# Second attention: where ScalarE's copy of the value products and VectorE's low parts and additions stand in a step

## The reference, cut to what matters

```
q = x @ Wq.T;  k = context @ Wk.T;  v = context @ Wv.T        # 16 heads of 16, context of 154 rows
scores = jnp.einsum('bhqd,bhkd->bhqk', q, k) * SCALE
scores = jnp.where(causal[None, None, :, :], scores, -jnp.inf) # causal = tril(1024 x 154)
probs = jax.nn.softmax(scores, axis=-1)
y = jnp.einsum('bhqk,bhkd->bhqd', probs, v)
return y.transpose(0, 2, 1, 3).reshape(b, t, c) @ Wo.T + bo    # then x + tanh(g) * this
```

## Time and profile before

| | us |
|---|---|
| median of 3 runs | 3179.37 (3177.24 to 3179.78) |
| the profiled execution | 3180.92 |
| its span | 3179.1 |
| second attention in it, first to last score | 2616.5 to 2942.2 |
| busy: PE, DVE, ACT, POOL | 3027.3, 2439.1, 1636.8, 718.9 |

### The profile page before, as it was taken

The page is one execution under the profiler, slowest core; times in us unless marked ns, Lnnn a source line. Parts: engine busy times, 40 slices in busy tenths (PEclk is TensorE's granted clock), DMA queues, the critical chain, the costliest instruction groups (busy, mean ns, idle before and its releaser), DMA issues. The chain is left out here.

```text
span 3179.1 us, 64710 instructions
## 1 busy us (share of the span) xinstructions
PE 3027.3 (95%) x21380; PEld 2785.9 (88%) x21380; DVE 2439.1 (77%) x4983; ACT 1636.8 (51%) x3099; POOL 718.9 (23%) x1290
## 2 busy tenths in 40 slices
PE   5999999999999999999989999999999988999688
PEld 5999999999999999999978888999999987777476
DVE  6777777777777777887876687878878768777797
ACT  3655555555555555555643332222222237777687
POOL 3232222322223322222101111111111122222220
PEclk9999999999999999999999999999999999999899
DMA  3000000000000000000020022334343320000001
GB/s 104 11 15 11 13 12 12 15 11 13 13 10 15 13 12 13 11 11 8 1 61 5 19 69 89 115 94 116 96 116 95 96 80 3 1 0 1 1 21 34
DMA packets 117392, 114.10 MB, mean 36 GB/s; under 512 B 39630, under 2 KB 83078, under 8 KB 117126
## 3 DMA queue, kind: packets, MB, share of 16 engines
q1 hardware_dynamic: 117126, 110.75, 12.1%
HBM read 105.46 MB, written 5.24 MB: 35 GB/s over the span
## 5 line engine op out<-in xcount | busy, mean ns | idle before, releaser
L454 ACT ACTIVATE x_pth<-x_ps 128x512 fp32r<-128x512 f32 (+1 forms) x768 | 375.9, 528 | 254.2 <-PE x_ps L751 251.6
L1107 ACT ACTIVATE moe_sil<-moe_ps,all_b 128x512 f32<-128x512 f32 x256 | 176.1, 688 | 543.8 <-PE moe_ps L1291 541.6
L555 DVE TENSOR_TENSOR x_ptl<-x_ps,x_pth 128x512 fp32r<-128x512 f32 (+1 forms) x768 | 402.9, 552 | 30.9 <-ACT x_pth L454 18.8
L474 ACT ACTIVATE all_buf<-all_buf,x_nmx 128x1178 f32<-128x1178 f32 x256 | 327.6, 1280 | 129.1 <-DVE all_buf L590 128.8
L590 DVE TENSOR_SCALAR_CACHE_REDUCE all_buf<-x_ps 128x1182 f32<-128x1182 f32 x256 | 354.5, 1385 | 22.3 <-PE x_ps L762 13.5
L1316 PE MATMUL moe_ps<-moe_w2z,moe_gh 128*128 128x256 f32 (+1 forms) x1280 | 369.4, 289 | 2.1 <-DVE moe_gl L1241 2.0
L751 PE MATMUL x_ps<-ident,all_buf 128*128 128x128 f32 x2560 | 365.3, 274 | 6.0 <-DVE x_ptl L555 5.9
L1316 PE MATMUL moe_ps<-moe_w2z,moe_gl 128*128 128x256 f32 x1280 | 362.8, 283 | 0.0
L1316 PE MATMUL moe_ps<-moe_w2l,moe_gh 128*128 128x256 f32 x1280 | 362.6, 283 | 0.0
L777 PE MATMUL x_ps<-x_pth,x_vh 128*128 128x256 f32 x1152 | 347.0, 301 | 0.0
L777 PE MATMUL x_ps<-x_ptl,x_vh 128*128 128x256 f32 x1152 | 325.9, 283 | 0.0
(11 more groups left out here) (383 smaller groups left out, 7897.9 us busy)
## 6 DMA issues: line engine op xcount, KB each, us to landing
moe_gate<-moe_cw_rows SPq DMA_DIRECT2D x512, 128.0 KB, 2.9
all_buf<-in_L_ffn_w_dram SPq DMA_DIRECT2D x16, 512.0 KB, 5.7
xres<-in_x_dram SPq DMA_DIRECT2D x4, 1024.0 KB, 10.3
x_rawk<-in_L_xattn_Wkv_dram SPq DMA_DIRECT2D x32, 128.0 KB, 2.2
x_rawq<-in_L_xattn_Wq_dram SPq DMA_DIRECT2D x32, 128.0 KB, 2.2
x_rawv<-in_L_xattn_Wkv_dram SPq DMA_DIRECT2D x16, 256.0 KB, 2.9
x_rawo<-in_L_xattn_Wo_dram SPq DMA_DIRECT2D x32, 128.0 KB, 2.0
out_dram<-xres SPq DMA_DIRECT2D x8, 512.0 KB, 2.9
```

The lines of the kernel that those rows point to most:

```text
L454: act.activation(turn_dst(pth, x, lo, hi), turn_src(x, g), ACT.Copy).then_inc(hi_done, 1)
L474: act.activation(p[:, w % 4, DUP:DUP + R_KV], p[:, w % 4, DUP:DUP + R_KV], ACT.Exp, bias=nmx[:, w % 2:w % 2 + 1], scale=-1.0, accum_out=su ...
L555: last = dve.tensor_tensor(turn_dst(ptl, x, lo, mid), turn_src(x, g)[:, 0:mid - lo, :], turn_dst(pth, x, lo, mid).bitcast(F32), ALU.subtract)
L1107: act.activation(dst[:, q % 2, :], ps[:, HID + q % 2, :], ACT.Silu, bias=bias).then_inc(silu_done, 1)
```

## The change

On ScalarE `keep` moves to the head of the step. On VectorE `maximum` 0, `divide`, `maximum` 1 and `kept` 1 move ahead of `x_part`, `q_part`, the addition and `o_part`; `kept` 2 stays behind them. No instruction is added or taken away.

```
 # ScalarE
             def step(b, w, before, after):
+                keep(b, behind(w, 3, 1, before))
                 if w % 4 == 0 and w < STEPS and (after or w + 4 < STEPS):
                     x_part(CPB * b + w // 4 + 1)
                 if w % 4 == 1 and w < STEPS and (after or w + 3 < STEPS):
                     q_part(CPB * b + w // 4 + 1, (w // 4 + 1) % 2)
                 o_part(b, behind(w, TURN_OUT + 1, 4, before))
-                keep(b, behind(w, 3, 1, before))
                 kept(b, behind(w, 1, 1, before), 0)
 # VectorE
             def step(b, w, before, after):
+                if w < STEPS:
+                    maximum(b, w, 0)
+                divide(b, behind(w, 3, 1, before))
+                if w < STEPS:
+                    maximum(b, w, 1)
+                kept(b, behind(w, 1, 1, before), 1)
                 if w % 4 == 0 and w < STEPS and (after or w + 4 < STEPS):
                     x_part(CPB * b + w // 4 + 1)
...
                 o_part(b, behind(w, TURN_OUT + 1, 4, before))
-                if w < STEPS:
-                    maximum(b, w, 0)
-                divide(b, behind(w, 3, 1, before))
-                if w < STEPS:
-                    maximum(b, w, 1)
-                kept(b, behind(w, 1, 1, before), 1)
                 kept(b, behind(w, 1, 1, before), 2)
```

More of the change, by code:

```diff
@@ L1825, in step @@
                 o_part(b, behind(w, TURN_OUT + 1, 4, before))
[L1826 to L1831, removed]
                 kept(b, behind(w, 1, 1, before), 2)
```

## The result

The changed kernel takes 3197.34 us (median of 6 runs, 3195.76 to 3198.23), the kernel before 3178.3 us in the same comparison (6 runs, 3176.28 to 3184.26). The ratio is 1.0054 with a 95% interval of 1.0044 to 1.0063: slower by 17 us, between 14 and 20. The forecast was slower by 9.2 us. The direction and the mechanism came as forecast, the size is nearly twice the forecast. The median lies 0.3 us above the upper end of the range of 3175 to 3197 us; taken by the ratio from the 3179.37 us that the forecast started from it is 3196.5 us, just inside.

The account below looks back on a forecast made before the run. TensorE was taken to set the pace; two waits go but longer new chains come: +11.5 us in the groups, -2.5 in the first ten steps, +0.2 in the last units, so +9.2 us, 3188.6 us, range 3175 to 3197.

Parts of the forecast that it names:

- The waits that go: TensorE's waits at `tokens` (10.5 us in the stage) and `values` (8.1) removed; 2.06 us off a plain group.
- the four new waits: TensorE behind VectorE's moved instructions: `turn_out` about 0.56 us, `x_turn` and `query` 0.50, `project` 1.20; 2.76 us a group.
- The chain: Last `score` 1 matmul, second maximum, copy, moved part, TensorE's start: 2.39 us in A and B, 2.45 D, 3.09 C.
- "3.09 in C": Chain length in step C, 1.70 us plus 1.39 for the query's low part; TensorE then waits 1.20 us.
- "1.74 us longer": A causal group, with four more score matmuls in each step, goes from 21.49 to 23.23 us.
- "SP and POOL see nothing": No transfer is issued by what moves, so SP and POOL (GpSimd) are unaffected.
- The 48 steps in sum: Eight plain groups 5.6 us, three causal 5.2, one D and A 0.9, one B and C -0.2: +11.5 us.
- The first ten steps: Steps 0 to 9 of the first batch: part of VectorE's 9.0 us of gaps goes, taken as 2.5 us.
- "Steps 10 to 17 of the last batch ... nothing changes": VectorE busy 29.82 of 30.54 us there, so it is the bound whatever the order.
- The rule for the other side: Skill's advice cited for the rival that waits go and nothing replaces them: 18.6 us less, 3161 us, chance 0.10.
- `keep` at the head "costs nothing": ScalarE's copy first in the step never waits long; ScalarE has 4.70 us of work in step C's 6.68.
- The clock: Rival: TensorE's clock falls behind the 1.20 us wait in 12 steps C, adding 24 us, 3212 us; chance 0.05.

Follow-up runs that it names:

- ScalarE's half: Kernel before with only ScalarE's `keep` copied first in the step, VectorE's order unchanged; 3184.9 us, ratio 1.0013 to the kernel before.
- VectorE's half: Changed kernel with ScalarE's order put back as before, VectorE's changed order kept; 3211.65 us, ratio 1.0094.
- parts ahead of maximum 1: Changed kernel with VectorE's low parts and additions placed between the division and the second maximum; 3161.53 us, ratio 0.9941.
- the kernel with the copy last: Changed kernel with VectorE's copy of 128x512 (`kept` 1) put behind the low part or addition; 3168.31 us, ratio 0.996.
- the run that holds GpSimd back: Changed kernel with GpSimd's third spreading of k in a batch held until VectorE's normalisation of that step ended; 3196.6 us, ratio 1.0049.
- the first pair: First profiles of the kernel before and the changed kernel, both profiled once more later; first ten steps 2.6 us shorter in this pair, 1.5 in the other.
- the best one: Changed kernel with VectorE's low parts and additions between the division and the second maximum; 3161.53 us, ratio 0.9941.
- the parts in the middle with ScalarE's order as before: Kernel with VectorE's parts between division and second maximum, ScalarE's order put back as in the kernel before; 3177.79 us, ratio 0.9995.

## Why the forecast was right in kind and short in size

Mean step lengths over the 48 steps, in us (number of steps; the last A is `w=15`):

| kernel | D (9) | A (6) | B (9) | C (9) | causal B, C, D, A (3 each) | A, w=15 (3) | 48 steps |
|---|---|---|---|---|---|---|---|
| before | 3.97 | 4.22 | 5.41 | 6.69 | 5.70, 6.68, 4.50, 4.61 | 4.22 | 247.12 |
| changed | 4.54 | 4.60 | 5.65 | 6.46 | 6.20, 7.02, 5.06, 5.16 | 5.05 | 263.01 |
| ScalarE's half | 4.01 | 4.36 | 5.60 | 6.69 | 5.78, 6.68, 4.50, 4.61 | 4.35 | 250.59 |
| VectorE's half | 4.54 | 4.77 | 5.82 | 7.37 | 6.20, 7.66, 5.06, 5.18 | 5.05 | 275.70 |
| parts ahead of maximum 1 | 3.96 | 4.13 | 5.14 | 5.08 | 5.70, 5.64, 4.50, 4.61 | 4.04 | 225.90 |

- **The waits that go, and the new ones.** Right. `tokens` and `values` wait for nothing in C, VectorE's 2.4 us ahead of the query part are gone, and the four new waits stand where they were put. The kernel with the parts ahead of the second maximum has none of the new ones in its 48 steps, and of the old ones a single wait of 0.2 us. It also shows how long the steps are when free of waits, and there the working was right: C 5.08 us (forecast 5.08), a causal group 20.45 (20.47). What was too small are the new chains.
- **The chain, link by link.** D was forecast at 2.45 us and is 2.46 (2828.13 to 2830.59), B 2.39 and is 2.39. Their steps grew by 0.57 and 0.24 us, against 0.56 and 0.21.
- **C is where the term was too small.** "3.09 in C" is 3.30, from 2842.91 to 2846.21, and so C gains 0.23 us and not 0.40. Two links were off. The query's low part was taken to start 0.60 us behind the copy, as other parts do; it starts 0.71 behind, just past the copy's full 0.68. In the kernel with the copy last it starts 0.83 behind the maximum of 0.80, where the low part of x starts 0.71 behind its own: this pair waits for the end of what is in front of it. The Trainium skill has that as a model (VectorE: DVE Perf Modes, Two Vector instructions with no wait between them): an instruction whose output begins in another group of 32 partitions than the last one's starts only when all before it have finished. The pair writes its halves crosswise, the first into partitions 64 to 127, and the trace agrees. The other link is from VectorE's end to TensorE's start, 0.05 us in B but 0.15 in C and in A (2835.06 to 2835.21), in each of the twelve steps of a kind. The trace shows what stands in between: in C an instruction of TensorE's sequencer (`PEldq`) that waits for semaphores, then the weight load (`PEld`), and in B the weight load alone.

```profile
L1988 PEldq EVENT_SEMAPHORE  x1: 51/51/51, 2846.1 to 2846.1; - x1
2846.18 0.19 PEld L1993 LDWEIGHTS x_ps<-x_woh,x_oh 128*128 128x128 f32 x1 [1.80 <-issue]
...
2839.72 0.19 PEld L2013 LDWEIGHTS x_ps<-x_xTh,x_wqh 128*128 128x128 f32 x1 [0.91 <-DVE x_xTl L1770]
```

`project` and `x_turn` wait for several semaphores. In the trace the one that comes last is waited for by the sequencer's instruction, and the weight load behind it carries a wait that was done long before; in `query` the weight load itself waits for VectorE. The price of 0.09 us was read from these steps; no run puts the waits in another order. Over nine steps C with 0.40 for 0.23: 1.6 us.
- **Causal groups.** "1.74 us longer" is 1.96, for the most part by the same links, in C and A. Three of them: 0.7 us.
- **"SP and POOL see nothing".** Wrong, and the one step whose mechanism failed within the 48 steps. No instruction of GpSimd changed its place, but VectorE's normalisation starts 0.5 us later in the step, and slid under one of GpSimd's. By the run that holds GpSimd back it costs 1.4 us in three steps A. With the 0.05 us that each A is over forecast besides (its chain is 2.49 us for 2.39, by the link above) the steps A make 1.8 us.
- **The 48 steps in sum:** +11.5 forecast, +15.9 measured: C 1.6, causal 0.7, A 1.8, D and B 0.4, which is the difference of 4.4 but for rounding.
- **The first ten steps:** -2.5 forecast, -1.5 at equal clock. That the first pair shows -2.6 is luck: 1.1 us of it are the lower clock in one step of one profile of the kernel before. Step `w=1`, which the forecast named, is 2.1 us shorter at equal clock and step `w=9` 0.9, but `w=2` is 1.6 us longer, which it did not have.
- **"Steps 10 to 17 of the last batch ... nothing changes".** Wrong: +1.25 us in the five steps looked at. VectorE was busy there for 21.01 of 21.53 us, but TensorE for 21.20 as well, so VectorE was not alone the bound. Now VectorE is busy for 21.31 of 22.78 us and TensorE for 20.77: with the new order gaps opened in both.
- **The rule for the other side** (the Trainium skill, Perfetto Trace Analysis, Optimization Strategy: make what the gaps of the most contended engine depend on start sooner) is no wrong aim: followed for both waits it takes 21.2 us out of the 48 steps, more than the 18.6 us that the two rows of waits show for the whole stage. What it leaves out is what becomes late. The changed kernel and the best one differ only in the order on VectorE.
- **`keep` at the head "costs nothing".** True in the changed kernel, where it is worth 12.7 us, and false in the kernel before, where it costs 3.5: whether the copy's 0.4 us matter is decided by what VectorE has queued behind the high part. The text gave only ScalarE's own load as a reason, and that does not bear the claim.
- **The clock** stayed at 1.00 in the 48 steps of both profiles of the changed kernel, with a gap of 1.35 us in each C. That rival is out here. A fall does occur in the stage: besides step `w=2` above, step `w=9` of the first batch was granted 0.86 in the one profile of ScalarE's half alone, behind a gap of 1.57 us, and 0.81 in that of the parts in the middle with ScalarE's order as before, behind one of 1.97 us. So sums of the first ten steps are to be compared at equal clock only.

## What to carry over

When work is moved back to let something else go first, add up the new chain from starts, link by link, and hold it against the time that the waiting engine needs on its own; of the places tried, the best for the short work was between the division, which TensorE awaits, and a maximum that nobody awaits soon. Price two halves of a change together and apart: each of these alone made the kernel slower, and at the right place they are worth 21 us of the stage. And look at what each moved instruction now lies beside, on engines that the change does not touch.

## What the runs showed of the hardware

A VectorE instruction from SBUF to SBUF (normalisation, 128x256 fp32, 0.40 us) took 1.30 us beside a GpSimd instruction of 1.26 us with two inputs in SBUF, and ended just behind it, while GpSimd's grew only from 1.22 to 1.26. A maximum, which reads PSUM, keeps its 0.79 us beside the next such GpSimd instruction (2787.26, under the one from 2787.16). The Trainium skill describes this as an exclusive lock on a pair of ports that VectorE and GpSimd share (SBUF — State Buffer, Who interferes with whom), taken by a VectorE instruction in a mode that uses both its ports or with two inputs in SBUF: who comes first holds it for a whole instruction. The trace agrees for the second of the two normalisations, which ended only behind GpSimd's instruction; in which mode it runs the trace does not say. I had not looked for this when I wrote that GpSimd sees nothing.
